# State-space layer between batches: TensorE projects x ahead of the last sums, and z behind dt and the transposes of normalised rows

## What is computed

```python
h = _ln(x, norm1_w, norm1_b) * (1.0 + s1) + sh1
def _mamba(h):
    x, z = jnp.split(h @ in_proj_W, 2, axis=-1)          # 512 channels each
    x = _silu(conv(x) + conv_b)                          # four taps along time
    xdbl = x @ x_proj_W
    dt = softplus(xdbl[..., :DT_RANK] @ dt_proj_W + dt_proj_b)
    Bm, Cm = ...                                         # 32 states
    hst = hst * exp(dt * A) + dt * Bm * x                # scan over 512 steps
    y = einsum('bdn,bn->bd', hst, Cm) + Dp * x
    return y * _silu(z) @ out_proj_W
x = x + g1 * (_mamba(h) + flip(_mamba(flip(h))))
h = _ln(x, norm2_w, norm2_b) * (1.0 + s2) + sh2
x = x + g2 * ((_silu(h @ w1) * (h @ w2)) @ w3)
```

## Time and profile before

| | us |
|---|---|
| median of 3 runs (6073.6 to 6080.58) | 6074.44 |
| the profiled execution | 6084.69 |
| its span in the trace | 6082.9 |
| PE busy | 5689.5 (94%) |
| DVE busy | 4381.9 (72%) |
| ACT busy | 4138.3 (68%) |
| POOL busy | 2794.2 (46%) |

### The profile page before, as it was taken

How to read it: one execution, slowest core, us unless ns; L and a number is a source line. 1 busy time by engine, 2 the same in 40 slices (tenths; PEclk the granted TensorE clock), 3 DMA queues, 4 the chain that set the end, 5 groups by cost and what they waited for, 6 DMA issues and landing times. The chain is left out here.

```text
span 6082.9 us, 76475 instructions
## 1 busy us (share of the span) xinstructions
PE 5689.5 (94%) x28272; PEld 2971.3 (49%) x28272; DVE 4381.9 (72%) x4793; ACT 4138.3 (68%) x6776; POOL 2794.2 (46%) x2152
## 2 busy tenths in 40 slices
PE   8999989999999998999997999999999999999998
PEld 5444445555555554454544444444444444444444
DVE  5766644434444435667674999989898998989897
ACT  3454545544455543445445989989898999989896
POOL 0000002222222221010001978969696987969696
PEclk8999999999999999999998999999999999999999
DMA  5223221000000004242323102020201102020200
GB/s 133 51 40 55 37 62 10 3 2 3 2 1 2 2 2 57 40 67 39 66 47 49 34 23 59 25 57 30 52 30 47 37 20 62 29 54 30 52 31 18
DMA packets 168724, 222.43 MB, mean 37 GB/s; under 512 B 37153, under 2 KB 104058, under 8 KB 168098
## 3 DMA queue, kind: packets, MB, share of 16 engines
q1 hardware_dynamic: 168354, 217.55, 16.6%
HBM read 152.90 MB, written 30.49 MB: 30 GB/s over the span
## 5 line engine op out<-in xcount | busy, mean ns | idle before, releaser
L2380 DVE TENSOR_TENSOR_SCAN l__h<-l__decay,psum 128x1024 f32<-128x1024 f32 x1024 | 2246.2, 2263 | 56.6 <-POOL l__hc L2358 22.1
L2358 POOL TENSOR_TENSOR l__hc<-l__h,l__c_rep 128x1024 f32<-128x1024 f32 x1016 | 2012.9, 2010 | 132.6 <-DMA l__c_rep<-l__c_dram 75.1
L1952 ACT ACTIVATE l__decay<-l__dt_rep,l__a_neg 128x511 f32<-128x511 f32 x2048 | 1341.7, 710 | 31.0 <-DVE l__h L2380 30.6
L1962 PEld LDWEIGHTS psum<-ident,l__dtx_B 128*128 128x128 f32 x8192 | 884.9, 141 | 902.7 <-DVE l__h L2380 605.5
L2483 PE MATMUL psum<-l__hc,l__gather 128*64 128x512 f32 x4096 | 1110.1, 620 | 141.3 <-POOL l__hc L2358 139.7
L1962 PE MATMUL psum<-ident,l__dtx_B 128*128 128x128 f32 x8192 | 1121.5, 280 | 71.3 <-DVE l__h L2380 45.0
L1936 ACT ACTIVATE l__dtx_B<-l__dtx_T,l__b_T 128x512 f32<-128x512 f32 x1664 | 1104.7, 711 | 5.0 <-PE psum L1962 2.9
L689 DVE TENSOR_REDUCE l__row_max<-psum 128x1 f32<-128x512 f32 x1024 | 655.7, 686 | 235.5 <-PE psum L704 234.8
L1411 POOL TENSOR_SCALAR l__probs<-l__probs,l__rec 128x512 f32<-128x512 f32 x512 | 350.1, 697 | 912.9 <-DVE l__rec L1407 912.8
L197 POOL TENSOR_SCALAR l__ln_var_eps<-l__ln_mean_var 128x4 f32<-128x4 f32 x57 | 16.4, 288 | 1577.5 <-DVE l__ln_mean_var L183 1577.5
L1037 ACT ACTIVATE l__probs<-psum 128x1024 f32<-128x1024 f32 x512 | 502.2, 1024 | 222.1 <-PE psum L1109 217.8
(11 more groups left out here) (170 smaller groups left out, 6496.6 us busy)
## 6 DMA issues: line engine op xcount, KB each, us to landing
l__c_rep<-l__c_dram SPq DMA_DIRECT2D x512, 128.0 KB, 2.9
l__dt_rep<-l__dt SPq DMA_DIRECT2D x128, 256.0 KB, 5.0
l__parts_dram<-l__parts SPq DMA_DIRECT2D x64, 384.0 KB, 3.4
l__q_stack<-l__parts_dram SPq DMA_DIRECT2D x192, 128.0 KB, 6.5
l__k_stack<-l__parts_dram SPq DMA_DIRECT2D x192, 128.0 KB, 9.2
l__w<-in_l_w SPq DMA_DIRECT2D x6, 1024.0 KB, 7.6
l__gate_rows<-l__gates_dram SPq DMA_DIRECT2D x24, 256.0 KB, 3.3
in_mod_w<-in_mod_w SPq DMA_DIRECT2D x1, 4608.0 KB, 17.1
```

Source lines behind the costliest of these rows:

```text
L1952: nc.scalar.activation(decay[:, i % DECAYS, s, 1:T], dt_rep[:, w, c, s, 1:T], ACT.Exp, scale=a_neg[:, g, c, s:s + 1]).then_inc(S["decay"], 1)
L1962: last = nc.tensor.transpose(bx_psum(i)[:, s, t * P:(t + 1) * P], dtx_B[:, (k + 1) % 2, t, 2 * c + s, :, :].rearrange("p j d -> p (j d)"), ...
L2358: nc.gpsimd.tensor_tensor(hc[:, i % HCS, :, :], h[:, i % HS, :, :], c_of(i), ALU.mult).then_inc(S["hc"], 1)
L2380: nc.vector.tensor_tensor_scan(both(h[:, i % HS, :, :]), both(decay[:, i % DECAYS, :, :]), both(bx_psum(i)), 0.0, ALU.mult, ALU.add).then_ ...
```

## The change

`silu_z(2)` and `silu_z(3)` move on ACT from before `softplus(0)` to after `softplus(3)`, ahead of `take_dtx_T(0)`. On PE `project_in(6)` and `(7)` move from between the x-projection and `project_dt(0)` to behind the MLP's `norm.tensor`, ahead of `fill_dtx_T(0)`. The waits follow: `project_dt(1)` no longer waits for z, `project_in(6)` waits for `softplus(1)`, and `fill_dtx_T(0)` waits until both `silu_z` are done. Apart from that, `project_in(0)` moves ahead of `y_sum(62)`. The first two moves are made in the stage before the first element too.

```diff
@@ -2117,8 +2117,6 @@
                     act.wait_ge(*S.at("dc_filled", w + 1))
                     nc.scalar.activation(dc[:, w, :], bank[DC_BANKS[w]][0:ROWS, :], ACT.Copy).then_inc(S["dc"], 1)
                 y_first(3)
-                silu_z(2)
-                silu_z(3)
                 softplus(0)
@@ -2130,6 +2128,8 @@
                 softplus(2)
                 softplus(3)
             if begin:
+                silu_z(2)
+                silu_z(3)
                 take_dtx_T(0)
             if end:
                 silu_up(0)
@@ -2181,8 +2181,6 @@
                 if c == 0:
                     pe.wait_ge(*S.at("dc", 2))
                     pe.wait_ge(*S.at("in_taken", 2 * IC - 2))
-                if c == 1:
-                    pe.wait_ge(*S.at("in_taken", 2 * IC))
@@ -2195,7 +2193,7 @@
             def fill_dtx_T(c):
                 pe.wait_ge(*S.at("dtx", c + 1))
                 if c == 0:
-                    pe.wait_ge(*S.at("dt", 2))
+                    pe.wait_ge(*S.at("in_taken", 2 * IC))
@@ -2226,8 +2224,6 @@
                 project_in(pe, IC + 1)
                 for c in range(IC):
                     project_x(c)
-                project_in(pe, IC + 2)
-                project_in(pe, IC + 3)
                 project_dt(0)
@@ -2241,6 +2237,9 @@
                     pe.wait_ge(*S.at("bT", 1))
                 norm.tensor(nc, pe, 1 if begin else 0, bank[6:8])
             if begin:
+                pe.wait_ge(*S.at("dt", 2))
+                project_in(pe, IC + 2)
+                project_in(pe, IC + 3)
                 fill_dtx_T(0)
@@ -2492,11 +2491,11 @@
             if begin:
                 pe.wait_ge(*S.at("scan", UNITS - 1))
                 norm.tensor(nc, pe, 0, bank[0:DC])
-            y_sum(UNITS - 2)
             if begin:
                 pe.wait_ge(*S.at("scan", UNITS))
                 pe.wait_ge(*S.at("hT", DC))
                 project_in(pe, 0)
+            y_sum(UNITS - 2)
             y_sum(UNITS - 1)
```

## The result

The changed kernel took 6110.73 us (median of 4 runs, 6105.79 to 6115.61) where the kernel before took 6077.51 (median of 4, 6073.6 to 6087.73). The ratio is 1.0053, with a 95% interval of 1.0038 to 1.0068: slower by 0.53%, 33 us, where 14.8 were forecast. The direction was right, but the loss is more than twice the forecast one, and the time lies above the stated range of 6082 to 6097.

The account below looks back on a forecast made before the run. The prediction took ACT as the full engine at the loop's start, passing each stage's loss on seven times. Seven stages at +2.05 (+14.4) plus +0.4 gave +14.8 on 6074.44, so 6089 us, range 6082 to 6097.

Parts of the forecast that it names:

- x ahead of the sums, +0.1: project_in(0) before y_sum(62): sooner projection worth nothing because DVE holds the convolution; +0.1 us a stage, 0 to +0.2.
- z taken out, −2.82: ACT after y_first(3): the Softplus load and softplus block start 2.82 us sooner, with PE keeping up.
- z put back, +1.95: Between softplus(3) and take_dtx_T(1): Silu load, silu_z and project_up(0) queued behind the fill make take_dtx_T(1) 1.95 us later.
- The loop passes it on: Unit loop: each stage's loss reaches the total seven times, counted in full because ACT is the full engine.
- the low bound of that term: Loop's start: takes off 0.17 us a stage, as POOL's first product moves less than the scan; seven stages +10.7.
- The stage before the first element, +0.4: Stage without up-projection: take_dtx_T(0) at 3286.3 instead of 3285.90, +0.4 us, bounds 0 to +1.
- PE's clock falls in the new hole: Rival, PE idle before fill_dtx_T(0): project_up(0) takes 3.6 us more a stage, +25 us, so 6114; chance 0.06.

Follow-up runs that it names:

- run 1: Only project_in(0) moved ahead of y_sum(62), z left in place, against the kernel before: 6081.69 us against 6078.48, ratio 1.0003.
- run 3: z moved without the swap of the sums, 16 unused transposes filling PE's hole before fill_dtx_T(0), against the kernel before: 6093.43 us against 6078.48, ratio 1.0024.
- run 6: The full change plus 16 unused transposes in PE's hole between z and fill_dtx_T(0), against the kernel before: 6101.6 us against 6087.7, ratio 1.0023.
- Run 4: z moved without the swap of the sums, z chunks 2 and 3 leaving PSUM by Copy instead of Silu: 6089.86 us in a single execution.
- run 5: z moved without the swap, project_up(0) before fill_dtx_T(0) and silu_up(0) before take_dtx_T(0), against the kernel before: 6091.45 us against 6087.7, ratio 1.0002.
- run 9: 14 zero-adding matmuls at the loop's end, in the kernel with z between the fills (0.9991) and the kernel before (1.0008), both against the kernel before.
- run 10: The changed kernel measured again, against the kernel before: 6113.91 us against 6084.62, ratio 1.0042.
- run 2: Only z moved, y_sum(62) kept ahead of project_in(0), against the kernel before: 6104.1 us against 6078.48, ratio 1.0039.
- run 7: The full change with 16 unused transposes in z's hole and 14 zero-adding matmuls at the loop's end, against the kernel before: 6104.74 us against 6087.7, ratio 1.0032.

## Why the prediction was wrong

**x ahead of the sums, +0.1:** measured +0.02 with the clock up (run 1). DVE holds the convolution as argued; the sooner first projection is worth nothing. What the step left out is that the gap of 1.25 us in front of `project_in(0)` can cost the clock, 1.65 us, all of which reaches ACT, because PE has no gap from there to the z chunk that ACT waits for. The step had just that chain in hand and used it only for 0.1 us.

**z taken out, −2.82:** right to 0.01. From the start of `y_first(3)` to the Softplus load it was 3.55 us and is 0.73. The MLP's rows came in time.

**z put back, +1.95:** +1.96 measured where the clock stays up (runs 3 and 6, and two stages of the change). The predicted idle time of 2.8 us before `silu_up(0)` is 2.79, the gap of 2.05 on PE is 2.16. Run 4 shows the Silu load in it (1.37 with its hand-over), run 5 the queue on PE (with `project_up(0)` first, +0.14 is left).

**The loop passes it on:** all but 0.17 us, which is just the 0.17 by which POOL's first product used to wait for the DMA of C; it is now released by the scan, as in the sixth stage of the changed kernel:

```profile
5420.74 2.00 POOL L2357 TENSOR_TENSOR l__hc<-l__h,l__c_rep 128x1024 f32<-128x1024 f32 x1 [10.91 <-DVE l__h L2379]
```

That speaks for POOL's start as what sets the loop's pace, not ACT's, though no run tests it; the low bound of that term was the right value.

**The stage before the first element, +0.4:** −0.3 (from the start of `y_first(3)` to the first scaling 15.36 us before and 15.03 now). PE's clock was down for a part of it before (0.93 on average from 3270 to 3290) and up now (1.00), so this difference isn't the change's alone.

**What failed is the clock's term: the rival "PE's clock falls in the new hole" was given 0.06 and left out of the sum, and the sum had no such term at the loop's end either.** Three things were wrong with it. Its evidence against was a single row, 8 matmuls at full speed behind 2.23 us of idle time. In run 6 and both kernels of run 9 the same eight behind the same 2.23 or 2.24 us took 5.40 us; in the other eleven profiles, 3.70. One row at full speed shows only that the clock can stay up, not that it does. The trace of before had rows that spoke the other way: the fall behind 1.14 us in its first stage, shown above, and three in the unit loops, at 3816.2, 4509.1 and 5202.0, each behind a gap of 1.90 us. Second, its place was taken to be the new gap alone; the other is at the loop's end. Third, its price, 3.6 us a stage, took the whole up-projection at half speed, where the clock is back up before its end: 1.69 (5.29 for 3.60), with 1.65 at the loop's end. Put together, a stage grows by 1.81, or by 5.14 where both places are slow: 7 × 1.81 = 12.7 to 7 × 5.14 = 36 us, with 28.8 in the first profile and 33 in the medians. The forecast was the lower end of this, and run 3 is the kernel that it describes: 6093 us, +15.

## What to carry to other kernels

When work is moved so that one engine waits for a whole round trip of another (here PE for softplus, a table load and two silus), price TensorE's new gap too: 1 to 2 us of idle time are worth up to another 1.7 us, if what comes behind is on the path. A row at full speed behind such a gap is no evidence that it is safe. Look for work to put into the gaps that are there, rather than making one elsewhere: the same z matmuls placed between the fills gained 0.9 us a stage where their clock held.

## What the runs showed of the hardware

- Behind a gap of only 1 to 2 us the granted clock can fall to 1.2 GHz, and it comes back while PE works on, a little over 3 us later. That is why 1.25 us of idle time cost more than they last. Behind z's gap it fell 1.0 to 1.3 us after PE had resumed (16 falls). At the loop's end it fell within the gap in 12 cases of 41, up to 0.55 us before PE resumed, up to 0.53 us after it in 22, and on the transposes ahead of that gap in 7. The Trainium skill, in "TensorE: Matmul & The Clock Gate", section "HAM oscillation — how this bites in real kernels", tells of loops in which an idle gap throttles the engine each time round; the traces agree, with gaps of only 1 to 2 us in an engine that is otherwise 92% busy.
- What a fall costs depends on what runs in it. The three falls in the unit loops of before go with steps of 346.47 to 346.57 us, against 346.41 to 346.45 without: 0.1 us, where a fall in the stage that hits a projection costs 1.65.
- Whether it falls at a given gap varies between stages with identical timing up to that point, and between runs of one kernel. It doesn't look random from stage to stage: `project_in(0)` was slow in 0 of 7 stages of run 3 and in 7 of 7 of run 10. In the 21 stages with both gaps open, 16 have a fall at both places, 4 at neither, and one (the first of run 2) at the loop's end alone; none has it at z alone. Either the two gaps meet the same alignment to something that the trace doesn't show, or the first fall brings on the second: in the changed kernel it moves the end of z's gap from 38.6 to 40.2 us behind the end of the first gap. No run tests either, and it stays open.
- Filling gaps with idle matmuls takes the fall away at its place (0 of 21 stages at the loop's end, 0 of 21 at z in runs 3, 6 and 7), but it costs when the fillers are a little longer than the gap: 0.9 to 1.0 us a round at the loop's end (runs 7 and 9), more than it saved.
- The table switch costs 1.37 us in the chain (run 4), one load of 1.28 and a hand-over. The extra drain that the Trainium skill gives in "ScalarE: Activation LUTs", section "What ACT_TABLE_LOAD costs", isn't seen here.
